# A decoder layer with eight experts: the last batch through all experts densely, and the last sorted group interleaved differently

## The reference, cut to what matters

```
p      = softmax(x2 @ gate_w.T)            # 8 experts
v, idx = top_k(p, 2)                       # two experts a token, weights v
y      = sum over the two of v * (relu(x2 @ w1[e] + b1[e]) @ w2[e] + b2[e])
out    = layernorm(x2 + y)                 # no scale or shift
```

## Time and profile before

| | us |
|---|---|
| median of 3 runs | 809.16 |
| lowest and highest | 800.09, 818.52 |
| the profiled execution | 808.52 |
| its span on the core | 806.7 |
| PE busy in the span | 647.5 (80%) |
| DVE, ACT, POOL busy | 468.5, 368.2, 283.4 |
| the chain that ended last, PE's part | 55% |

### The profile page before, as it was taken

One profiled execution on the slowest core, in us unless ns is written; L12 is line 12 of the kernel. 1 busy time (PEld: TensorE's weight loads), 2 busy tenths in 40 slices (PEclk: granted clock), 3 DMA queues, 4 the chain that ended last, 5 costly groups with the idle time before them and its releaser, 6 DMA issues.

```text
span 806.7 us, 18948 instructions
## 1 busy us (share of the span) xinstructions
PE 647.5 (80%) x6549; PEld 497.2 (62%) x6549; DVE 468.5 (58%) x1730; ACT 368.2 (46%) x1283; POOL 283.4 (35%) x464
## 2 busy tenths in 40 slices
PE   5468988988998899869988997898899956762650
PEld 4345765675677678636776776576767845661650
DVE  2539538857974886557748766786566542431110
ACT  4344535545464665244646654554355432330230
POOL 0437214603921360359012601694400044305123
PEclk9768758985999999556999999898899966996795
DMA  4080300013044212040343241404342214665540
GB/s 141 12 306 2 100 1 2 19 70 109 21 133 128 91 38 87 24 141 8 114 129 109 75 152 40 148 16 168 118 120 73 74 66 153 204 187 165 158 129 23
DMA packets 47703, 77.71 MB, mean 96 GB/s; under 512 B 8240, under 2 KB 35064, under 8 KB 46456
## 3 DMA queue, kind: packets, MB, share of 16 engines
q1 hardware_dynamic: 45560, 72.30, 28.5%
q0 software_dynamic: 2048, 4.20, 1.6%
HBM read 64.45 MB, written 12.03 MB: 95 GB/s over the span
## 4 chain that ended last, share of the span: by engine, by line
PE 55%; issue 14%; DVE 14%; ACT 8%; POOL 6%; DMA 1%; SPq 0%; another core or an unknown queue 0%; DVEq 0%; POOLq 0%; ACTq 0%
PE bM L787 8%; PE bG L932 6%; PE bH L1159 6%; PE bR L1133 5%; PE bW L1133 4%; PE bM L975 4%; ACT ht L1373 4%; PE bS L951 3%; PE bM L980 3%; PE bC L1032 2%; PE bW L787 2%; PE bS L948 2%; PE bR L1064 2%; PE bG L1159 2%; PE bC L787 2%
## 5 line engine op out<-in xcount | busy, mean ns | idle before, releaser
L1373 ACT ACTIVATE ht<-bH,wt 128x128 f32<-128x128 f32 x216 | 61.5, 369 | 75.0 <-PE bH L1159 70.9
L1291 ACT ACTIVATE pp<-pp,nmx 128x224 f32<-128x224 f32 x96 | 46.4, 484 | 81.7 <-DVE nmx L1549 81.3
L1555 DVE TENSOR_TENSOR gs<-bG,rank_t 96x512 f32<-96x512 f32 x96 | 65.5, 682 | 15.1 <-PE bG L932 14.5
L1303 ACT COPY pts<-bM 128x256 f32<-128x256 f32 x96 | 35.4, 368 | 63.2 <-PE bM L787 62.8
L1618 DVE TENSOR_TENSOR sm<-bC,cst 128x512 f32<-128x512 f32 x64 | 43.6, 682 | 34.9 <-PE bC L1081 33.4
L1159 PE MATMUL bH<-xt,wt 128*128 128x128 f32 x432 | 62.8, 293 | 0.1
L932 PE MATMUL bG<-oh,kspl 128*96 128x512 f32 x160 | 61.3, 467 | 0.0
L693 POOL TENSOR_TENSOR r<-x,cst 128x256 f32<-128x256 f32 x8 | 5.8, 724 | 156.5 <-DVE x L1582 156.5
L1159 PEld LDWEIGHTS bH<-xt,wt 128*128 128x128 f32 x432 | 58.8, 209 | 1.0 <-issue 0.4
L1537 DVE TENSOR_SCALAR ppn<-pp,rls 128x224 f32<-128x224 f32 (+1 forms) x128 | 48.2, 376 | 14.1 <-DVE rls L1534 0.5
L975 PE MATMUL bM<-pts,ckw 96*32 96x64 f32 x512 | 52.4, 292 | 4.0 <-ACT ots L1311 4.0
(11 more groups left out here) (272 smaller groups left out, 1622.3 us busy)
## 6 DMA issues: line engine op xcount, KB each, us to landing
wt<-in_experts SPq DMA_DIRECT2D x67, 578.0 KB
sidx<-far_slots SPq DMA_DIRECT2D x8, 1536.0 KB, 6.6
xs<-sorted_tokens SPq DMA_DIRECT2D x67, 64.0 KB
expert_rows<-ot SPq DMA_DIRECT2D x67, 64.0 KB, 3.4
sorted_tokens<-acc SPq DMA_DIRECT2D x13, 256.0 KB, 7.7
cst<-shape_constants SPq DMA_DIRECT2D x1, 1603.5 KB, 6.3
xn<-in_x SPq DMA_DIRECT2D x8, 128.0 KB, 5.6
xr<-in_x SPq DMA_DIRECT2D x8, 128.0 KB, 3.3
```

The costliest lines, as they stand in the source:

```text
L1291: AC(pp[:, s % 2, 0:w], bS[:, 0:w] if s < T0 else pp[:, s % 2, :], ACT.Exp, scale=1.0 if s < T0 else -1.0, bias=nmx[:, s % 2:s % 2 + 1], a ...
L1373: last = AC(ht[:, t % 2, f, :], w[:, 128 * f:128 * f + 128], ACT.Relu, bias=wt[:, t % NW, FF + f:FF + f + 1])
L1555: TT(gs[:, g % 2, :].rearrange("p (t j) -> p t j", j=FAR), bG[0:96, :].rearrange("p (t j) -> p t j", j=FAR), rank_t[:, :].rearrange("p (o ...
```

## The change

Three edits that belong together.

1. Group 4 is gone. There are 56 tiles in place of 67. Batch 7 (DENSE) has no list, no scatter and no gather. After the last slot, `dense(e)` takes its 256 tokens through each expert: PE's first product is four of 128x256 from the turned tokens x2T into bH and bG, ACT writes relu into hs, PE's second product is eight of 128x128 into bW, and DVE adds bias and product, each times the token's gate for that expert (`gg`, zero where the expert isn't one of its two), into `accd`. The router of batch 7 makes `gg` in place of the counts. The norm of batch 7 is on DVE alone. hs lies in a half of qall and accd in one of xr that are no longer used.
2. The weights of expert e go through the same ring as tile 56 + e. SP asks for experts 0 to 3 at tiles 12 to 15 of group 3, and for 4 to 7 in the dense part, each when its slot is free.
3. Group 3's tiles stand in slots 7 to 19 of step 8, with the half slots 9.5, 11.5, 13.5, 15.5 and 17.5 (`END_SLOTS`), all within the step. At PE q = 0 has the first product of tile k+1 and the turn of k+2, q = 1 the second product of tile k; ACT's relus move to q = 0 too.

Batches 5 and 6 are gathered after `dense(1)`, summed at `dense(4)` and `dense(6)` and finished one later.

```diff
-GROUPS = tuple((b, most_tiles(b)) for b in ((0,), (1, 2), (3, 4), (5, 6), (7,)))
+GROUPS = tuple((b, most_tiles(b)) for b in ((0,), (1, 2), (3, 4), (5, 6)))
+DENSE = NB - 1
...
+END_SLOTS = (0, 1, 2, 3, 7, 8, 9, 9.5, 10, 11, 11.5, 12, 13, 13.5, 14, 15, 15.5, 16, 17, 17.5, 18, 19)
...
-            here = next(p for p in free if p >= (batches[-1] + 2, FIRST_SLOT if batches[-1] + 2 < NB else 4))
+            here = next(p for p in free if p >= (batches[-1] + 2, FIRST_SLOT))
...
+                    if (step, s + 0.5) in TILE_AT:
+                        tile(*TILE_AT[step, s + 0.5], 0)
+                        tile(*TILE_AT[step, s + 0.5], 1)
...
-            g = len(GROUPS) - 1
-            tile_list(g)
...
+            late = [n for n in range(DENSE) if GROUP_OF[n] == ALONE]
+            for e in range(NE + 1):
+                dense(e)
+                if e == 1:
+                    for n in late:
+                        collect(n)
+                if e in (4, 6):
+                    summed(late[e // 2 - 2])
+                if e in (5, 7):
+                    normed(late[e // 2 - 2])
+            dense_end()
...
+            def load_expert(e):
+
+                t = TILES + e
+                if e < NW:
+                    sp.wait_ge(t_out.sem, t_out.at(t - NW, 1))
+                else:
+                    sp.wait_ge(e_out.sem, e_out.at(e - NW, 1))
+                sp.dma_start(wt[:, t % NW, :], io["experts"][e]).then_inc(d_wt[t % NW].sem, 16)
...
+                    elif g == ALONE and k + NW - 1 >= n:
+                        load_expert(k + NW - 1 - n)
...
+            def dense(e):
+                if 0 < e and e + NW - 1 < NE:
+                    load_expert(e + NW - 1)
...
+                else:
+                    if q == 0 and 0 <= k + 1 < n:
+                        first(g, k + 1)
+                    if q == 0 and k + 2 < n:
+                        turn_rows(g, k + 2)
+                    if q == 1 and 0 <= k < n:
+                        second(g, k)
+
+            def dense(e):
+                if e < NE:
+                    t = TILES + e
+                    pe.wait_ge(d_wt[t % NW].sem, d_wt[t % NW].at(t // NW, 16))
+                    for half in range(2):
+                        if e == 0:
+                            pe.wait_ge(t_h.sem, t_h.at(TILES - 1, 1))
+                        else:
+                            pe.wait_ge(e_h.sem, e_h.at(e - 1, half + 1))
+                        w = (bH, bG)[half]
+                        for f in range(2):
+                            lo = 256 * half + 128 * f
+                            last = MM(w[:, 256 * f:256 * f + 256], wt[:, t % NW, lo:lo + 128], x2T[:, :], start=True, stop=True)
+                        last.then_inc(e_first.sem, 1)
+                if e >= 1:
+                    u = e - 1
+                    t = TILES + u
+                    pe.wait_ge(e_h.sem, e_h.at(u, 2))
+                    if u < 2:
+                        pe.wait_ge(t_out.sem, t_out.at(TILES - 1, 1))
                     else:
+                        pe.wait_ge(e_out.sem, e_out.at(u - 2, 1))
+                    for r in range(2):
+                        for f in range(4):
+                            last = MM(bW[u % 2][:, 128 * r:128 * r + 128], hs[:, u % 2, f, 128 * r:128 * r + 128],
+                                      wt[:, t % NW, W2_AT + 128 * f:W2_AT + 128 * f + 128], start=(f == 0), stop=(f == 3))
+                    last.then_inc(e_second.sem, 1)
...
+            def dense(e):
+                if e < NE:
+                    if e >= 2:
+                        act.wait_ge(e_second.sem, e_second.at(e - 2, 1))
+                    t = TILES + e
+                    for half in range(2):
+                        act.wait_ge(e_first.sem, e_first.at(e, half + 1))
+                        w = (bH, bG)[half]
+                        for f in range(2):
+                            b = FF + 2 * half + f
+                            last = AC(hs[:, e % 2, 2 * half + f, :], w[:, 256 * f:256 * f + 256], ACT.Relu, bias=wt[:, t % NW, b:b + 1])
+                        last.then_inc(e_h.sem, 1)
...
+                if i.n == DENSE:
+                    gates(i, k)
+                    return
...
+            def dense(e):
+                if e == 0:
+                    dve.wait_ge(r_gate.sem, r_gate.at(0, 1))
+                if e < NE:
+
+                    t = TILES + e
+                    dve.wait_ge(d_wt[t % NW].sem, d_wt[t % NW].at(t // NW, 16))
+                    for r in range(2):
+                        before_ = x2[:, DENSE, r, :] if e == 0 else accd[:, r, :]
+                        k = oe.did(STT(accd[:, r, :], wt[:, t % NW, B2_AT:], gg[:, r, e:e + 1], before_, ALU.mult, ALU.add))
+                    oe.wait(k)
+                if e >= 1:
+                    u = e - 1
+                    dve.wait_ge(e_second.sem, e_second.at(u, 1))
+                    for r in range(2):
+                        k = oe.did(STT(accd[:, r, :], bW[u % 2][:, 128 * r:128 * r + 128], gg[:, r, u:u + 1], accd[:, r, :], ALU.mult, ALU.add))
+                    oe.wait(k)
+                    dve.sem_inc(e_out.sem, 1)
+
+            def dense_end():
+                dve.wait_ge(f_ln.sem, f_ln.at(DENSE - 1, 2))
+                summed_rows(DENSE, accd[:, :, :])
+                dve.wait_ge(f_rs.sem, f_rs.at(DENSE, 1))
+                root(of, fln, f_root)
+                dve.wait_ge(f_root.sem, f_root.at(DENSE, 1))
+                for r in range(2):
+                    TS(accd[:, r, :], accd[:, r, :], fmv[:, r, 0:1], fln[:, 5, r:r + 1], ALU.subtract, ALU.mult).then_inc(e_ln.sem, 1)
```

More of the change, by code:

```diff
@@ L62 @@
 LIST_SLOT, FIRST_SLOT = 2, 6
+END_SLOTS = (0, 1, 2, 3, 7, 8, 9, 9.5, 10, 11, 11.5, 12, 13, 13.5, 14, 15, 15.5, 16, 17, 17.5, 18, 19)
 def plan():
[L67 to L68 removed]
+    at, free = {}, [(step, s) for step in range(2, NB) for s in TILE_SLOTS] + [(NB, s) for s in END_SLOTS]
+    for g, (batches, most) in enumerate(GROUPS):
         for k in range(-2, most + 1):
[L70 removed]
+            here = next(p for p in free if p >= (batches[-1] + 2, FIRST_SLOT))
             free.remove(here)
@@ L74, in plan @@
     gather, first, second = {}, {}, {}
-    for n in range(NB):
+    for n in range(DENSE):
         g = GROUP_OF[n]
-        if g in ends and ends[g][0] < NB or g == 2:
+        if g < ALONE:
             step, s = ends[g]
@@ new lines, in second @@
+            def second(g, k):
+                t = tile_no(g, k)
+                pe.wait_ge(t_h.sem, t_h.at(t, 1))
+                if g < ALONE:
+                    emptied_r()
+                    w = bR
+                    held["second"] = t
+                else:
+                    w = bW[t % 2]
+                    if t >= 2:
+                        pe.wait_ge(t_out.sem, t_out.at(t - 2, 1))
+                for f in range(4):
+                    last = MM(w[:, 0:128], ht[:, t % 2, f, :], wt[:, t % NW, W2_AT + 128 * f:W2_AT + 128 * f + 128],
+                              start=(f == 0), stop=(f == 3))
+                last.then_inc(t_second.sem, 1)
@@ L1163, in collect, with dense_end @@
+            def dense_end():
+                pass
             def collect(n):
```

144 lines of the change are left out of this document (73 added, 71 removed).

## The result

| | before | after |
|---|---|---|
| median of the runs, us | 812.4 (4 runs) | 782.5 (4 runs) |
| ratio, 95% interval | | 0.9706, 0.9631 to 0.9781 |
| profiled execution, us | 808.5 | 776.2 |
| its span | 806.7 | 774.4 |

What follows compares the result with a forecast made beforehand. It took the serial PE-ACT chain of 3.39 us a tile as the bound, then the weight ring. 806.7 - 4.4 - 56.3 - 11.8 + 31.5 = 765.7, plus 1.8 and 0.6, made 768 us; range 754 to 784.

Steps and rivals of the forecast that it cites:

- Nothing changes before 662 us: Everything ahead of the last step: earlier groups planned as before, so only the last 145 us count.
- Part 1: Start of group 3: its first product starts at about 679 us instead of 672.1, 7 us later.
- Tile 2 at 688: Group 3: tile 2's first product at 688 instead of 684.4, behind DVE's wait for batch 3's sum.
- Part 2: Group 3, first product ahead of second: weight ring sets the pace, dense part begins at 725, gain 4.4 us.
- I take 2.4 us a tile: Group 3's tile period once the ACT wait goes; bounds 1.9 (PE) and 3.4 us (nothing gained).
- the same wait for batch 4's output costs 2 us: SP's in-order queue in group 3: weight loads wait for batch 4's output, costing 2 us.
- 297 GB/s of a backlog: DMA rate of queued loads and stores with engines at 0.94 for 7 us, giving 2.33 us a tile.
- Rival (b): Group 3: product swap gives nothing, tiles stay near 3.4 us; 777, or 781 with DVE and ACT held; chance 0.24.
- Part 3: Batch 7 dense: 56.3 us removed, eight experts at 3.56 us added (28.5) plus 3 us of stalls.
- The stalls: Dense part: gathers of batches 5 and 6 not fully covered, 3 us in all, bounds 0 and 8.
- Part 4: Tail from last second product to end: 9.2 us, 5.5 of it after the output's issue; 11.8 us less.
- The sum: Whole span: 806.7 - 4.4 - 56.3 - 11.8 + 31.5 = 765.7 us, a gain of 41.

Runs made afterwards that it cites:

- e_sumlate: Changed kernel with sums and norms of batches 3 and 4 three slots later in every engine's order; one run, 106.5 us from batch 5's first scatter to the end.
- e_oldslots: Changed kernel with group 3 back in its old slots (from slot 4, one tile a slot), new product order kept; ratio 0.947 to the kernel before.
- e_outlate: Changed kernel with SP's stores of the outputs of batches 3 and 4 moved to the start of the dense part; ratio 0.951 to the kernel before.
- e_storefirst: Changed kernel with SP asking for the last tiles' stores ahead of the dense experts' loads; ratio 0.945 to the kernel before.
- e_half: Changed kernel, batch 3 and 4 output stores in the dense part, group 3 weight loads from tile 3 cut to 578 columns; one run, 101.4 us from scatter to end.
- e_noswap: Changed kernel with group 3's second product ahead of the next first product again, new slots kept; ratio 0.960 to the kernel before.
- e_poolearly: Changed kernel with POOL adding up batch 6 before it scales batch 5; ratio 0.945 to the kernel before.
- e_denseonly2: Second run of the changed kernel with group 3's old slots and old product order, only batch 7 dense; ratio 0.954 to the kernel before.
- e_best2: Changed kernel with all helpful edits combined, plus sums and norms of batches 3 and 4 three slots later; ratio 0.944 to the kernel before.
- e_gatherlater: Changed kernel with POOL's gathers of batches 5 and 6 behind dense expert 3 in program order; one run, 115.9 us from batch 5's first scatter to the end.
- e_denseonly: Changed kernel with group 3's old slots and old product order, only batch 7 dense, first run; ratio 0.954 to the kernel before.

## Why the prediction was right or wrong

**Nothing changes before 662 us.** Right, up to the shift of 4.1 us that all parts share.

**Part 1.** Right: 679 predicted, 682.8 - 4.1 = 678.7; tile 5 at 697.3, measured 696.3. Tile 2 at 688, measured 686.7, is luck: it was put down to DVE's wait for the sum of batch 3, and without that wait (e_sumlate) it starts at the same time. PE's own work at the 1.2 GHz level sets it. The late slots' cost of 7 us at tile 0 was seen, but not that it stays to the end: e_oldslots begins its dense part 7.0 us earlier.

**Part 2.** Here the prediction failed: "I take 2.4 us a tile" with "the same wait for batch 4's output costs 2 us". From tile 5 to tile 14 it had 24.7 us, and they took 30.6; the dense part began at 730.3 (unshifted) where 725 was said. The bound was put on bandwidth, 297 GB/s of a backlog. In its place:
- SP's waits. The two were foreseen, the second at 2 us. Without them the dense part begins 6.6 us earlier (e_outlate): 3.8 are the waits, 2.8 the clock, which this part of the prediction took as full (e_storefirst).
- DVE's order. The router was given 1.0 us, the norm of batch 7 and the moments of batch 4 nothing; the waits for xt are 0.94 and 1.25 us behind these two, and 0.71 behind the router, or 1.36 where weights no longer hide it (e_half).
- Bandwidth. Half the bytes are worth 3 us in all (e_half).

The Trainium skill (DMA: Bandwidth & Descriptors, Specifications and Anatomy of one DMA — SWDGE (gpsimd) path) would have a weight load at 3.4 us by estimate, and the ring hardly binding. The fit is for transfers that GpSimd issues, and these are SP's; the two loads behind SP's waits took 4.1 and 4.3 us from issue to use, with others in flight.

Rival (b), the swap gives nothing, came closest in its number (period 3.4). Of its reasons the hole on SP held; its name did not: e_noswap shows a gain of 4 us or more by the swap, which the slots take back.

**Part 3.** The expert was right: 3.56 predicted, 3.51 measured, with 256-column passes at twice the 128-column ones (four of them start 0.86 us apart). The stalls were 3 us and are 6.0 (34.1 - 8 x 3.51). Tile 14's store was to land 4 us after its issue, and took 5.2 (735.31 to 740.47); the rest is order on POOL (the last wait goes from 2.02 to 0.50 us in e_poolearly) and the stall without a name.

**Part 4.** Too long: 9.2 predicted, 5.9 measured. The term that failed is "from the output's issue at 801.19 to the end at 806.7, 5.5": it is 2.3 in every profile with the dense part. Before, the last 3.7 us of the span hold no transfer any more; what fills them isn't known.

**The sum.** 5.3 late at the dense part, 2.6 more in it, 3.3 less in the tail: 4.6 less gain than the 41, which is the 36.4 of the profile. That the two misses of 7.9 us together show as 4.6 is luck of the tail. The rest, from 36.4 down to the first set's 24, isn't in these stages and stays open; runs of equal kernels differ by several us ahead of the change. Over all sets, 0.959 of 809.2 is 776.

## What to carry to other kernels

When work is pipelined more tightly, ask first what in-order queues wait for other engines in that stretch: a store that waits for a slow engine, ahead of loads in the same queue, costs nothing while there is slack and then all of its wait, and, in five of the six profiles with after's group 3, a stretch at TensorE's lower clock on top. An edit that hides one wait and one that delays the start can cancel; measure each alone. A backlog's rate is the bound only if the DMA engines stay full in the stretch itself. And read the granted clock of both profiles before a difference between them is put down to an edit.

## What the runs showed of the hardware

Behind idle times of 2.4 and 2.95 us inside an otherwise busy stretch, TensorE was granted 0.72 and 0.57 of its clock over the next 6 and 4 us; with no idle time over 1.25 us (e_outlate) it kept 1.00. It isn't the length of one pause that decides: e_storefirst kept 1.00 behind 2.54 and 2.79 us, e_poolearly in its dense part behind 2.76, and e_denseonly2 had 0.50 from 686.9 to 690.3 with no pause over 1.84 us in the 10 us before.

With eight indirect gathers in a row on POOL, ACT and DVE went on late behind finished products, ACT by 2.3 to 4.5 us and once by 7.3 (e_best2), in 11 of 16 such rows over these profiles. In seven of the 11 ACT went on 2.5 to 2.8 us after the eighth gather had started, in the others sooner. In the 32 rows of four the most was 1.7 us, once, on DVE (e_gatherlater, an ot); a few others have about 1 us. That the gathers cause it isn't shown: five rows have the eight and no stall, among them that of e_sumlate in group 3 and one of the two profiles of e_denseonly, the same kernel. What holds the engines back stays open.
